# A decoder on one Trainium2 core: in the first attention, masks and sinks are copied into the score banks by ACT and VectorE

## The chip, the core and the metric

The kernel runs on one core of a Trainium2 chip, as one program. The metric is device time in microseconds of one execution; the median of several runs is compared. Engines are named as in the profile: PE is the matmul engine (PEld its weight loads), DVE is VectorE, ACT is ScalarE, POOL is GpSimd, SP issues DMAs.

## What is computed

Two decoder layers on x of shape (8, 112, 512), each with a self-attention, a cross-attention and a feed-forward part, all with a layer norm ahead and a residual. The change concerns the self-attention of the first layer only:

```python
H, KV, D = (32, 8, 64)
G = H // KV
WINDOW = 64
...
scale = D ** (-0.5)
scores = jnp.einsum('bhqd,bhkd->bhqk', q, k) * scale
i = jnp.arange(Tq)
mask = (i[None, :] > i[:, None]) | (i[:, None] - i[None, :] >= WINDOW)
scores = jnp.where(mask[None, None], -jnp.inf, scores)
sink_col = jnp.broadcast_to(sinks[None, :, None, None], (Bq, H, Tq, 1))
combined = jnp.concatenate([scores, sink_col], axis=-1)
probs = jax.nn.softmax(combined, axis=-1)[..., :-1]
out = jnp.einsum('bhqk,bhkd->bhqd', probs, v)
```

So a row of scores has 112 keys, of which some are masked, and one extra column, the head's sink.

## The kernel before, in words

The program is written engine by engine. Each engine runs its own list of stages in order (projections, first attention, its output projection, cross-attention and so on), and instructions wait on semaphores that count in the order of the engine that raises them. `done(...)` names a point that an instruction raises, `upon(...)` a point that is waited for. An engine has one counter for a stage, so `act_a0` counts all of ACT's points in the first attention.

**Tiling of the first attention.** There are U0 = 32 units of eight heads for one batch element, and W0 = 16 rounds w of two units, 2w and 2w+1 (a batch element takes two rounds). The score banks are PSUM banks 0 to 3: unit 2w uses banks 0 and 1, unit 2w+1 banks 2 and 3. Each bank holds four heads with 114 columns each, 112 scores and two columns for the sink (the softmax reads the first of them). Banks 4 and 5 take transposed probabilities, 6 and 7 the value products. So there is one set of score banks: round w+1 can touch them only after the exp of round w has read them.

**A round on PE** (`pe_att0`). `scores(w)` first writes the mask into each of the four banks (L532, an identity matmul with start=True, which overwrites), waiting for the exp of the unit that used the bank last (L531). Then come eight matmuls with one row each that put the sinks, split into a high and a low part, into the two last columns (L536), and 64 products of 32 rows, Q by K (L542), which add to the mask. After the scores PE transposes unit 2w-3 (`turn`, eight transposes, L260), makes the value products of unit 2w-4 (`values`, L566), subtracts the row maxima of unit 2w from its banks with two matmuls (`less`, L550), transposes unit 2w-2, subtracts those of unit 2w+1, and makes the value products of unit 2w-3. In rounds 0 and 1 some value projections (L255 to L257) stand between. The order of this list is fixed by hand.

**The other engines.** DVE takes the maxima of both units (`largest`, L650), then the sums of the exps (`sums`, L655, and a reciprocal, L657), for the even unit in its own round and for the odd one at the start of the next. ACT raises exp (`power`, L612) into SBUF tiles Sk, copies transposed probabilities to SBUF (`turned`, L604) and value products to QO (`out`, L618); in rounds 2 and 3 it also rounds a weight piece (L296) between the two exps. POOL multiplies Sk by the reciprocals (`share`, L677). Before the stage, `dve_proj0` scales the sinks by 8, copies a row of ones and splits the sinks into skh and skl; ACT copies the identity (`one`, L621) and the mask (`maskR`, L622) to fp32r tiles for PE. The value add of the projection stage is L398.

The last two rounds (w = 16, 17) make no scores; they finish the transposes and value products. Then the output projection (L255 to L257) follows on PE.

Of the kernel before, what the change touches and what calls it, by code (L numbers as in the profile page):

```python
# [8 lines left out]
F = mybir.dt.float32  # L9
# [66 lines left out]
def build(nc, g):  # L76
# [8 lines left out]
    with ExitStack() as ctx:  # L85
# [56 lines left out]
        ones = misc("ones", [128, S], R)  # L142
        skh = misc("skh", [S, 32], R)
        skl = misc("skl", [S, 32], R)
# [290 lines left out]
        def dve_proj0(e):  # L435
# [25 lines left out]
            e.tensor_scalar(M("sinks", S), M("sinks", S), 8.0, None, A.mult).then_inc(*done("dve_p0", "sinks8"))  # L461
            e.tensor_copy(ones[:, :], C("ones")[:, 0:S]).then_inc(*done("dve_p0", "ones"))
            e.wait_ge(*upon("dve_p0", "sinks8"))
            e.tensor_copy(skh[:, :], M("sinks", S)).then_inc(*done("dve_p0", "skh"))
            e.wait_ge(*upon("dve_p0", "skh"))
            e.tensor_tensor(skl[:, :], M("sinks", S), skh[:, :].bitcast(F), A.subtract).then_inc(*done("dve_p0", "sinks"))
# [42 lines left out]
        def sinks_of(part, w, i):  # L509
            row = part[32 * i:32 * i + 1, :].rearrange("p (s h i) -> p s i h", s=2, h=4)[:, w % 2, i, :]  # L510
            return row.unsqueeze(2).to_broadcast([1, 4, 2])
# [15 lines left out]
        def pe_att0(e):  # L527
            def scores(w):
                b, s = w // 2, w % 2
                for i in range(4):  # L530
                    e.wait_ge(*(upon("act_a0", "exp", 2 * w - 2 + i // 2) if w else upon("dve_p0", 16 + i // 2, i % 2)))  # L531
                    e.matmul(bank0(i)[:, :, 0:S], one[0:S, 0:S], maskR[:, :].unsqueeze(1).to_broadcast([S, 4, S]), start=True,  # L532
                             stop=True)
                for part in (skh, skl):
                    for i in range(4):
                        e.matmul(bank0(i)[:, :, S:S + 2], ones[32 * i:32 * i + 1, :], sinks_of(part, w, i), start=False, stop=True,  # L536
                                 skip_group_check=True)
                for h in range(4):
                    for ab in range(2):
                        for i in range(4):  # L540
                            p = slice(32 * i, 32 * i + 32)
                            last = e.matmul(bank0(i)[:, h, 0:S], QO[p, 1 + w, 2 * h + ab, :],  # L542
                                            Kt[p, 2 * s + ab, b * S:(b + 1) * S], start=False, stop=True, skip_group_check=True)
                            if h == 3 and ab == 1:
                                last.then_inc(*done("pe_a0", "sc", w, i))
# [25 lines left out]
            e.wait_ge(*upon("act_a0", "mask"))  # L571
            e.wait_ge(*upon("dve_p0", "sinks"))
# [26 lines left out]
        def act_att0(e):  # L599
# [20 lines left out]
            e.wait_ge(*upon("pe_ln", "x", NT - 1))  # L620
            e.activation(one[:, :], C("ident"), ACT.Copy)  # L621
            e.activation(maskR[:, :], C("mask0", S), ACT.Copy).then_inc(*done("act_a0", "mask"))  # L622
            for w in range(W0 + 2):
# [9 lines left out]
                if w < W0:  # L633
                    power(2 * w + 1)
                if 0 < w <= W0:
                    turned(2 * w - 2)
# [7 lines left out]
        def dve_att0(e):  # L644
# [6 lines left out]

            def sums(u):
# [5 lines left out]

            for w in range(W0 + 1):
                if w:  # L660
                    sums(2 * w - 1)
                if w < W0:
                    largest(2 * w)
                    largest(2 * w + 1)
                    if w < 2:
                        value0_out(e, 6 + w)
                    sums(2 * w)
# [1909 lines left out]
```

## Time and profile before

| | us |
|---|---|
| median of 3 runs | 1678.25 |
| lowest and highest | 1677.41 and 1680.61 |
| the profiled execution, its time | 1680.23 |
| its span, first to last instruction | 1678.4 |
| PE busy | 1602.4 |
| DVE busy | 991.4 |
| ACT busy | 730.2 |
| POOL busy | 508.6 |

The span is read from the profile, which is one execution; its busy times overlap, since the engines work side by side. The first attention runs from 138.2 us (its first mask matmul) to about 267 us, where the output projection's matmuls begin. A row of the timeline merges instructions of one kind that follow each other: its duration is that of the group, and its count stands behind the x.

### The profile page before, as it was taken

The numbers are of one execution on the slowest core, as the hardware profiler recorded it, in microseconds if no ns is written. First come the engines' busy times: TensorE is split into PE (matmuls) and PEld (weight loads), VectorE is DVE, ScalarE is ACT, GpSimd is POOL, SyncE is SP. The second block draws the span as 40 slices with busy tenths as digits, with TensorE's granted clock in tenths as the row PEclk, the third lists the DMA queues.
The fourth block names the chain that finished last, engine by engine and source line by source line (L and its number), as shares of the span: only waits on it lengthen the run. The fifth ranks groups of instructions, "written<-read, shape, count | busy, mean of one in ns | idle before, by whom it ended". The sixth has DMA issues, their size and how long they took to land.

```text
span 1678.4 us, 24116 instructions
## 1 busy us (share of the span) xinstructions
PE 1602.4 (95%) x9668; PEld 1329.3 (79%) x9668; DVE 991.4 (59%) x1658; ACT 730.2 (44%) x1221; POOL 508.6 (30%) x335
## 2 busy tenths in 40 slices
PE   7999999999899999989999989999889999999998
PEld 6897667778688888867889987787677888878887
DVE  5555663455676675487758748244757455554555
ACT  2113664223577765666611146422635334353442
POOL 3875542520100002331117734111611432212321
PEclk9999999999999999999999999999999999999999
DMA  4110003134312004410001110110001111111111
GB/s 164 53 61 28 2 2 130 39 99 130 106 53 64 13 1 161 156 38 1 1 1 63 50 39 1 44 43 32 21 14 44 51 53 55 51 45 51 51 57 44
DMA packets 28578, 88.49 MB, mean 53 GB/s; under 512 B 4154, under 2 KB 4282, under 8 KB 28215
## 3 DMA queue, kind: packets, MB, share of 16 engines
q1 hardware_dynamic: 28468, 86.96, 15.6%
q8 instruction: 77, 1.26, 0.3%
q14 instruction: 33, 0.27, 0.1%
HBM read 85.11 MB, written 1.84 MB: 52 GB/s over the span
## 4 chain that ended last, share of the span: by engine, by line
PE 85%; DVE 8%; ACT 4%; issue 1%; POOL 0%; DMA 0%; ACTq 0%; DVEq 0%
PE PS L255 18%; PE PS L257 17%; PE PS L256 17%; PE PS L260 6%; PE PS L1026 5%; PE PS L1044 4%; PE PS L1376 3%; PE PS L932 3%; PE PS L1391 2%; PE PS L542 2%; PE PS L566 1%; PE PS L1623 1%; PE PS L1611 1%; PE PS L532 1%; DVE sm L1645 1%
## 5 line engine op out<-in xcount | busy, mean ns | idle before, releaser
L301 POOL TENSOR_TENSOR HL<-stg,HL 128x1024 fp32r<-128x1024 f32 (+2 forms) x111 | 244.0, 2201 | 824.2 <-ACT HL L296 803.8
L255 PE MATMUL PS<-XT,HL 128*128 128x448 f32 x608 | 225.3, 371 | 7.5 <-DVE XT L336 5.3
L257 PE MATMUL PS<-XT,HL 128*128 128x448 f32 x608 | 223.5, 368 | 0.0
L256 PE MATMUL PS<-XT,HL 128*128 128x448 f32 x608 | 223.5, 368 | 0.0
L296 ACT ACTIVATE HL<-stg 128x1024 fp32r<-128x1024 f32 (+2 forms) x111 | 104.2, 943 | 217.8 <-PE PS L257 202.5
L255 PE MATMUL PS<-HL,XT 128*128 128x512 f32 (+1 forms) x380 | 138.6, 365 | 3.7 <-DVE rs L316 1.6
L257 PE MATMUL PS<-HL,XT 128*128 128x512 f32 (+1 forms) x380 | 135.4, 356 | 0.0
L256 PE MATMUL PS<-HL,XT 128*128 128x512 f32 (+1 forms) x380 | 135.3, 356 | 0.0
L255 PEld LDWEIGHTS PS<-XT,HL 128*128 128x128 f32 x608 | 115.0, 189 | 19.1 <-DVE XT L336 6.0
L256 PEld LDWEIGHTS PS<-XT,HL 128*128 128x128 f32 x608 | 115.0, 189 | 9.7
L257 PEld LDWEIGHTS PS<-XT,HL 128*128 128x128 f32 x608 | 114.9, 189 | 9.8
L2197 DVE SCALAR_TENSOR_TENSOR Hh<-PS,sml,Hh 128x448 fp32r<-128x448 f32 x64 | 43.8, 684 | 114.2 <-ACT Hh L2085 114.2
L1026 PE MATMUL PS<-kvT,QO 128*112 128x375 f32 x256 | 93.2, 487 | 6.4 <-DVE kvT L816 5.6
L255 PE MATMUL PS<-HL,Ph 128*128 128x512 f32 x224 | 90.4, 404 | 5.4 <-DVE x L2227 1.8
L706 DVE TENSOR_TENSOR XT<-QO,XT 128x896 fp32r<-128x896 f32 x32 | 36.8, 1159 | 98.3 <-ACT XT L700 98.3
L1090 DVE TENSOR_REDUCE nm<-PS 112x2 f32<-112x750 f32 x64 | 60.1, 939 | 52.4 <-PE PS L1026 52.4
L256 PE MATMUL PS<-HL,Ph 128*128 128x512 f32 x224 | 87.5, 391 | 0.0
L257 PE MATMUL PS<-HL,Ph 128*128 128x512 f32 x224 | 87.5, 391 | 0.0
L2085 ACT ACTIVATE Hh<-PS,sml 128x448 fp32r<-128x448 f32 x64 | 40.6, 634 | 105.7 <-PE PS L257 105.7
L1044 PE MATMUL PS<-PX,kvr 125*128 125x224 f32 x384 | 84.2, 355 | 0.0
L255 PEld LDWEIGHTS PS<-HL,XT 128*128 128x128 f32 (+1 forms) x380 | 70.9, 187 | 16.0 <-issue 3.5
L257 PEld LDWEIGHTS PS<-HL,XT 128*128 128x128 f32 (+1 forms) x380 | 70.7, 186 | 10.4
(283 smaller groups left out, 3603.2 us busy)
## 6 DMA issues: line engine op xcount, KB each, us to landing
stg<-in_wst SPq DMA_DIRECT2D x87, 512.0 KB, 3.5
stg<-in_wst SPq DMA_DIRECT2D x16, 352.0 KB, 3.1
stg<-in_wst SPq DMA_DIRECT2D x16, 320.0 KB, 3.8
wsum<-in_wfc SPq DMA_DIRECT2D x8, 512.0 KB, 4.1
wsum<-in_wpj SPq DMA_DIRECT2D x8, 512.0 KB, 3.6
raw<-in_wfc SPq DMA_DIRECT2D x8, 512.0 KB, 6.7
stg<-in_wst SPq DMA_DIRECT2D x16, 256.0 KB, 2.6
raw<-in_wpj SPq DMA_DIRECT2D x7, 512.0 KB, 7.0
```

The lines of the kernel that those rows point to most:

```text
L255: e.matmul(out, lh, rh, start=start, stop=False)
L256: e.matmul(out, lh, rl, start=False, stop=False)
L257: return e.matmul(out, ll, rh, start=False, stop=stop)
L260: return e.transpose(out, in_, C("ident", n)[:, 0:n])
L296: e.activation(slot(k)[:, 0, 0:n], stg[k % NSTG][:, 0:n], ACT.Copy).then_inc(*done("act_w", k))
L301: e.tensor_tensor(slot(k)[:, 1, 0:n], stg[k % NSTG][:, 0:n], slot(k)[:, 0, 0:n].bitcast(F), A.subtract).then_inc(*done("pool_w", k))
L932: last = e.matmul(out, Mhl[i][:, a, kc, :], XT[:, c, kc, hs], start=kc == 0 and j == 0, stop=kc == 3 and j == 2)
L1026: last = e.matmul(PS[0:S, bank + e_, 0:L], QO[:, 1 + st // 4, 2 * (st % 4) + e_, :], kvT[:, b, :], start=True, stop=True)
L1044: last = e.matmul(PS[:, 6 + u % 2, 0:2 * S], kvr[:, c, u // 4 % 8, :], PX[u % 2][:, :, c, :], start=c == 0, stop=c == 2)
L1090: e.tensor_reduce(nm[:, st % 4, :], PS[0:S, bank:bank + 2, 0:L], AX.X, A.max, negate=True).then_inc(*done("dve_x", "nm", st))
L1376: last = e.matmul(PS[:, 7, :], YT[c4][:, hl, kc, :], w_rows(ter, 1, c4 * 4 + kc), start=c4 == 0 and kc == 0 and hl == 0, stop=c4 == 3 and ...
L2197: e.scalar_tensor_tensor(out=half_of(Hh[:, 1, ch, :], h), in0=PS[:, 2 * h + ch, 0:HT], scalar=M("bup")[:, 2 * n + ch:2 * n + ch + 1], in1= ...
```

## The change

The mask and the sinks are no longer put into the score banks by PE. ACT and DVE copy them there, in fp32, from the constant table (mask0) and from the scaled sinks: DVE banks 0 and 1 for the even unit, ACT banks 2 and 3 for the odd unit. A fill is two instructions, one of 896 elements a partition (2 banks, 4 heads, 112 columns) and one of 16 (the sink columns). It waits for the exp that read the banks last. In ACT's list it stands right behind the exp of the odd unit, ahead of the copy of transposed probabilities; in DVE's list behind the maxima of its round, ahead of the sums of the even unit. The score products wait for both fills, and are to add to what they find in the banks. Only once, ahead of round 0, PE writes all 456 columns of each of the four banks with start=True (`clear`); the first fills wait for that. The matmuls for masks and sinks go, and with them the tiles ones, skh and skl, DVE's instructions that made them, and ACT's copy of the mask.

```diff
--- before.py
+++ after.py
@@ -139,9 +139,6 @@
         rsl = misc("rsl", [P, 2, 8])
         nmr = misc("nmr", [S, 4, 8], R)
         one = misc("one", [128, 128], R)
-        ones = misc("ones", [128, S], R)
-        skh = misc("skh", [S, 32], R)
-        skl = misc("skl", [S, 32], R)
         nm = misc("nm", [S, 4, 2])
         sx = misc("sx", [S, 4, 2])
         rx = misc("rx", [S, 4, 2])
@@ -458,12 +455,7 @@
                     ln_lo(e, "x", t, t)
             rope0(e, 2)
             rope0(e, 3)
-            e.tensor_scalar(M("sinks", S), M("sinks", S), 8.0, None, A.mult).then_inc(*done("dve_p0", "sinks8"))
-            e.tensor_copy(ones[:, :], C("ones")[:, 0:S]).then_inc(*done("dve_p0", "ones"))
-            e.wait_ge(*upon("dve_p0", "sinks8"))
-            e.tensor_copy(skh[:, :], M("sinks", S)).then_inc(*done("dve_p0", "skh"))
-            e.wait_ge(*upon("dve_p0", "skh"))
-            e.tensor_tensor(skl[:, :], M("sinks", S), skh[:, :].bitcast(F), A.subtract).then_inc(*done("dve_p0", "sinks"))
+            e.tensor_scalar(M("sinks", S), M("sinks", S), 8.0, None, A.mult).then_inc(*done("dve_p0", "sinks"))
             for u in range(4, 20):
                 rope0(e, u)
             value0_out(e, 4)
@@ -506,9 +498,17 @@
 
         U0, W0, U1 = 32, 16, 16
 
-        def sinks_of(part, w, i):
-            row = part[32 * i:32 * i + 1, :].rearrange("p (s h i) -> p s i h", s=2, h=4)[:, w % 2, i, :]
-            return row.unsqueeze(2).to_broadcast([1, 4, 2])
+        def sinks_of(u):
+            i = 2 * (u % 2)
+            sk = M("sinks", S).rearrange("p (s h i) -> p s i h", s=2, h=4)[:, u // 2 % 2, i:i + 2, :]
+            return sk.unsqueeze(3).to_broadcast([S, 2, 4, 2])
+
+        def mask_of():
+            return C("mask0", S).unsqueeze(1).unsqueeze(1).to_broadcast([S, 2, 4, S])
+
+        def whole0(u):
+            i = 2 * (u % 2)
+            return PS[0:S, i:i + 2, 0:4 * S + 8].rearrange("p i (h k) -> p i h k", h=4)
 
 
         def keys(ap, h=4):
@@ -527,14 +527,8 @@
         def pe_att0(e):
             def scores(w):
                 b, s = w // 2, w % 2
-                for i in range(4):
-                    e.wait_ge(*(upon("act_a0", "exp", 2 * w - 2 + i // 2) if w else upon("dve_p0", 16 + i // 2, i % 2)))
-                    e.matmul(bank0(i)[:, :, 0:S], one[0:S, 0:S], maskR[:, :].unsqueeze(1).to_broadcast([S, 4, S]), start=True,
-                             stop=True)
-                for part in (skh, skl):
-                    for i in range(4):
-                        e.matmul(bank0(i)[:, :, S:S + 2], ones[32 * i:32 * i + 1, :], sinks_of(part, w, i), start=False, stop=True,
-                                 skip_group_check=True)
+                e.wait_ge(*upon("dve_a0", "fill", 2 * w))
+                e.wait_ge(*upon("act_a0", "fill", 2 * w + 1))
                 for h in range(4):
                     for ab in range(2):
                         for i in range(4):
@@ -568,8 +562,11 @@
                 last.then_inc(*done("pe_a0", "pv", u))
 
             e.wait_ge(*upon("pool_p0", 19, 1))
-            e.wait_ge(*upon("act_a0", "mask"))
-            e.wait_ge(*upon("dve_p0", "sinks"))
+            e.wait_ge(*upon("act_a0", "one"))
+            for i in range(4):
+                e.wait_ge(*upon("dve_p0", 16 + i // 2, i % 2))
+                e.matmul(bank0(i), one[0:S, 0:S], one[0:S, 0:S + 2].unsqueeze(1).to_broadcast([S, 4, S + 2]), start=True,
+                         stop=True).then_inc(*done("pe_a0", "clear", i))
             for w in range(W0 + 2):
                 if w < W0:
                     scores(w)
@@ -617,9 +614,16 @@
                 g = 4 * (u % 2)
                 e.activation(QO[:, u // 2, g:g + 4, :], psv(6 + u % 2), ACT.Copy).then_inc(*done("act_a0", "o", u))
 
-            e.wait_ge(*upon("pe_ln", "x", NT - 1))
-            e.activation(one[:, :], C("ident"), ACT.Copy)
-            e.activation(maskR[:, :], C("mask0", S), ACT.Copy).then_inc(*done("act_a0", "mask"))
+            def fill(u):
+                if u > 1:
+                    e.wait_ge(*upon("act_a0", "exp", u - 2))
+                e.activation(whole0(u)[..., 0:S], mask_of(), ACT.Copy)
+                e.activation(whole0(u)[..., S:S + 2], sinks_of(u), ACT.Copy).then_inc(*done("act_a0", "fill", u))
+
+            e.activation(one[:, :], C("ident"), ACT.Copy).then_inc(*done("act_a0", "one"))
+            e.wait_ge(*upon("dve_p0", "sinks"))
+            e.wait_ge(*upon("pe_a0", "clear", 3))
+            fill(1)
             for w in range(W0 + 2):
                 if w > 1:
                     turned(2 * w - 3)
@@ -632,6 +636,8 @@
                     o_hi(e, "o0", 0)
                 if w < W0:
                     power(2 * w + 1)
+                if w < W0 - 1:
+                    fill(2 * w + 3)
                 if 0 < w <= W0:
                     turned(2 * w - 2)
                 if w >= W0:
@@ -649,6 +655,12 @@
                 e.wait_ge(*upon("pe_a0", "sc", u // 2, 2 * (u % 2) + 1))
                 e.tensor_reduce(nmr[:, k, :], unit0(u), AX.X, A.max, negate=True).then_inc(*done("dve_a0", "mx", u))
 
+            def fill(u):
+                if u:
+                    e.wait_ge(*upon("act_a0", "exp", u - 2))
+                e.tensor_copy(whole0(u)[..., 0:S], mask_of())
+                e.tensor_copy(whole0(u)[..., S:S + 2], sinks_of(u)).then_inc(*done("dve_a0", "fill", u))
+
             def sums(u):
                 k = u % 4
                 e.wait_ge(*upon("act_a0", "exp", u))
@@ -656,12 +668,16 @@
                 e.wait_ge(*upon("dve_a0", "sum", u))
                 e.reciprocal(rc[:, k, :], sm[:, k, :]).then_inc(*done("dve_a0", "rc", u))
 
+            e.wait_ge(*upon("pe_a0", "clear", 1))
+            fill(0)
             for w in range(W0 + 1):
                 if w:
                     sums(2 * w - 1)
                 if w < W0:
                     largest(2 * w)
                     largest(2 * w + 1)
+                    if w < W0 - 1:
+                        fill(2 * w + 2)
                     if w < 2:
                         value0_out(e, 6 + w)
                     sums(2 * w)
```

## Rows read from the trace of the kernel before

**Rows 1.** The page's first part: busy us of each engine.
```profile
PE 1602.4 (95%) x9668; PEld 1329.3 (79%) x9668; DVE 991.4 (59%) x1658; ACT 730.2 (44%) x1221; POOL 508.6 (30%) x335
```

**Rows 2.** Windows: stretch, length, busy us by engine (instructions), granted clock, DMA.
```profile
177.00:251.16 74.16, 74.16 (x1042) 49.73 (x1040) 45.91 (x61) 45.06 (x61) 33.25 (x20) 1.00 0.01 2
1210.00:1220.00 10.00, 8.14 (x131) 6.13 (x131) 7.21 (x12) 7.03 (x10) 4.03 (x3) 1.00 0.01 2
1220.00:1230.00 10.00, 5.51 (x88) 4.32 (x88) 2.31 (x4) 4.40 (x6) 3.32 (x2) 0.83 0.01 2
```

**Rows 3.** Timeline of one steady round: start us, duration, engine, line, operation, idle before.
```profile
208.01 1.81 PE L542 MATMUL PS<-Kt,QO 32*112 32x112 f32 x64
...
209.97 2.11 DVE L650 TENSOR_REDUCE nmr<-PS 112x8 fp32r<-112x904 f32 x2 [1.57 <-PE PS L542]
...
212.04 0.93 PE L260 MATMUL PS<-cst,Sk 112*112 112x112 f32 x8
212.30 0.92 ACT L612 ACTIVATE Sk<-PS 112x904 f32<-112x904 f32 x1
...
212.74 0.62 PE L550 MATMUL PS<-nmr,one 112*112 112x456 f32 x2
213.26 1.09 DVE L655 TENSOR_REDUCE sm<-Sk 112x8 f32<-112x904 f32 x1 [1.19 <-ACT Sk L612]
...
213.46 0.92 ACT L612 ACTIVATE Sk<-PS 112x904 f32<-112x904 f32 x1 [0.23 <-PE PS L550]
...
214.19 1.07 PE L532 MATMUL PS<-maskR,one 112*112 112x448 f32 x4
214.28 0.91 ACT L604 ACTIVATE PT<-PS 112x896 f32<-112x896 f32 x1
214.39 0.20 DVE L657 RECIPROCAL rc<-sm 112x8 f32<-112x8 f32 x1
214.51 1.04 DVE L655 TENSOR_REDUCE sm<-Sk 112x8 f32<-112x904 f32 x1
214.67 3.32 POOL L677 TENSOR_TENSOR Sk<-Sk,rc 112x896 f32<-112x896 f32 x2 [4.06 <-DVE rc L657]
...
215.41 1.81 PE L542 MATMUL PS<-Kt,QO 32*112 32x112 f32 x64
215.58 0.21 DVE L657 RECIPROCAL rc<-sm 112x8 f32<-112x8 f32 x1
```

**Rows 4.** Groups by form: copies on ACT and DVE; busy us, mean ns, idle before.
```profile
L700 ACT ACTIVATE XT<-QO 128x896 fp32r<-128x896 f32 x32 | 30.2, 950 | 74.5 <-PE PS L257 74.4
...
L621 ACT ACTIVATE one<-cst 128x128 fp32r<-128x128 f32 x1 | 0.3, 292 | 0.0
...
L1105 DVE COPY QO<-PS 128x224 f32<-128x224 f32 x64 | 25.1, 392 | 5.3 <-PE PS L1044 4.6
...
L1000 DVE COPY QO<-PS 128x448 f32<-128x448 f32 x16 | 9.3, 615 | 0.4 <-PE PS L954 0.4
L1461 DVE TENSOR_SCALAR Gb<-Gb,rs 128x2048 f32<-128x2048 f32 x7 | 9.0, 1286 | 0.2
```

**Rows 5.** Timeline of the start, round 0 and the end of round 2.
```profile
138.19 0.97 PE L532 MATMUL PS<-maskR,one 112*112 112x448 f32 x4
138.38 0.69 DVE L398 TENSOR_TENSOR V<-PS,bv 112x512 f32<-112x512 f32 x1 [2.14 <-PE PS L257]
...
139.31 1.81 PE L542 MATMUL PS<-Kt,QO 32*112 32x112 f32 x64
...
144.56 1.74 ACT L612 ACTIVATE Sk<-PS 112x904 f32<-112x904 f32 x2 [9.03 <-PE PS L550]
...
147.16 1.81 PE L542 MATMUL PS<-Kt,QO 32*112 32x112 f32 x64
...
161.44 0.92 ACT L612 ACTIVATE Sk<-PS 112x904 f32<-112x904 f32 x1
...
163.21 1.81 PE L542 MATMUL PS<-Kt,QO 32*112 32x112 f32 x64
```

## Prediction

> **What bounds the kernel now.** I read the page's head first: PE is busy 1602.4 of 1678.4 us and nothing else comes near it [rows 1]. That says only that PE matters on average, so I went to the stage that the change edits, the first attention. The windows view of its steady stretch, 177.00 to 251.16 us, shows PE busy all 74.16 us, at granted clock 1.00, while DVE is busy 45.9 and ACT 45.1 [rows 2]. So in these rounds PE never rests, and work taken off it is worth something, until another thing ends the round.
>
> What that other thing is has to be read from one round, in the timeline [rows 3]. A round w starts with its score products (208.01) and the next round's start at 215.41: 7.40 us. Count from 208.01 as zero. PE issues the 64 score products, eight transposes, four value products, the two matmuls that take off unit 2w's maxima, eight more transposes (212.04), and then, at 4.73, the two for unit 2w+1 (212.74 in the row). They last 0.62. ACT then makes exp(2w+1) from 5.45 to 6.37 (213.46, 0.92 long). PE in the meantime does value products, and at 214.19, 6.18 on this scale, begins the four mask matmuls of the next round, then the sinks' eight, then the scores. The masks of the banks that exp(2w+1) read can be written just after that exp ended at 214.38, so the exp-to-scores link is 215.41 - 214.38 = 1.03 us. The mask and sink matmuls fill this link almost completely. The round has two limits that lie close together: PE's list, 7.40 long, and the loop scores, maxima, subtraction, exp, bank ready, scores, which is just as long because the bank is made ready inside it.
>
> **The change part by part.**
>
> Removed from PE: 12 matmuls in each of 16 rounds, 215.41 - 214.19 = 1.22 us a round, 19.5 us in all. PE's own list falls to about 6.2 us. If PE alone set the pace, this would be the gain.
>
> Added to the loop: the fill. The bank pair of unit 2w+1 may be written only after exp(2w+1) has read it, and the scores of round w+1 wait for the copy. Before, the same bank pair was made ready by PE after the same exp; now it is made ready by ACT after it. The wait that vanishes (PE on its own list) is replaced by PE waiting for two ACT copies.
>
> Price of ACT's two copies. No row before shows ACT writing a score bank. The nearest rows are ACT copies of the same size from SBUF to SBUF, 896 elements in 950 ns, and one of 128 in 292 ns [rows 4]: 0.857 ns an element, so 16 elements take 292 - 112 x 0.857 = 196 ns. Two ACT instructions without a wait between them overlap: exp starts at 213.46, the next at 214.28, 0.82 later, though it lasts 0.92 [rows 3]. So the pair takes 0.95 - 0.10 + 0.20 = 1.05 us. An engine sees another's or its own end 0.04 later (exp(2w) ends 213.22, DVE starts 213.26; a sum ends 214.35, its reciprocal starts 214.39 [rows 3]). The new link is 0.04 + 1.05 + 0.05 = 1.14 us against 1.03. I take SBUF-to-SBUF as the price because the source is SBUF. Low bound: the big copy like the 0.82 that a PSUM read of that size occupies, the small one at half its estimate, 0.10: link 1.01. High bound: no overlap and a small copy as dear as the 128-element one: 0.95 + 0.29 + 0.09 = 1.33.
>
> [...]
>
> Added to DVE: a copy pair a round for unit 2w+2. The nearest rows are copies of 448 elements in 615 ns and 224 in 392 [rows 4], 0.996 ns an element: 896 take 1.06 us and 16 take 0.18, 1.25 together. The low bound is the paired pace of the 2048-element row, 1286 ns or at most 0.63 ns an element, some 0.75 for both. It starts after exp(2w), at 5.25, and is done at 6.5, a full microsecond before ACT's. Queued behind it on DVE are the sums of unit 2w, their reciprocals and the sums of 2w+1, which took 213.26 to 215.78 (two reduces, 1.13 and 1.07 with their gaps, and a reciprocal each); now they end at 6.5 + 2.5 = 9.0, that is 1.5 into the next round, and the first maxima reduce is wanted at 1.96 (209.97) [rows 3]. Slack 0.46. POOL's shares (3.32 for two) start at 7.8 in place of 6.66 (214.67) and end 11.1; PE transposes the first of them in the next round at 7.5 + 4.0 = 11.5 (212.04 is that place in the row). So DVE's fill costs nothing; it would need to last 1.7 us before it did.
>
> Queued behind ACT's fill are the copy of transposed unit 2w-2 (214.28 in the row) and an output copy: they move 1.1 later, to end about 1.3 into the next round. The first of them is wanted by PE at 1.8, when its scores are out. Nothing.
>
> Steady rounds: the 11 from 4 to 14 grow by 1.14 - 1.03 = 0.11, together 1.2 us.
>
> The four transitions before these lose more, since there the link was shorter: in round 0 both exps end at 144.56 + 1.74 = 146.30 and the scores start at 147.16, 0.86; in round 2 a weight copy on ACT pushes exp to 161.44, it ends 162.36, scores start 163.21, 0.85 [rows 5]. I take 0.86 for all four: 4 x (1.14 - 0.86) = 1.1 us.
>
> The start. Four new matmuls of 456 columns replace the first four of the masks, 138.19 to 139.16 [rows 5]: no change. But now the fills stand between them and the first scores, which before started at 139.31. ACT can start at 139.2, and is done at 140.3; DVE first finishes the value add (138.38 + 0.69) and is done at about 140.35. Scores start at 140.4: 1.1 us later, once. ACT's table load for Exp moves behind the first fill and ends long before the first exp at 144.56, so it is hidden. The three small DVE instructions that go (two copies and a subtract) lie in the projection under PE's work: nothing.
>
> The last round has no fill behind it, so the tail is as before. Sum: 1.2 + 1.1 + 1.1 = +3.4 us. The profiled execution has a span of 1678.4 and took 1680.23, so it would become 1681.8 and 1683.6; the median of the runs, 1678.25, lies 2.0 below that execution, and becomes 1681.7. All of the 19.5 us turns into PE waiting.
>
> **The rivals.**
>
> B, the short link: ACT's writes cost their low bound, 1.01. Then 11 x -0.02 + 4 x 0.15 + 0.9 = 1.3 us, 1679.6, not slower. It decides on where the pair takes under 0.95. For it: ACT reads PSUM faster than SBUF. Against: the source stays SBUF. Chance 0.17. [...]
>
> C, the clock: PE now rests 1.2 us in every 7.5, 83% busy. Where PE was 81% busy the clock still stood at 1.00, where it was 55% busy it was 0.83 [rows 2]. Should it be 0.83 here, PE's 5.4 us inside the loop stretch by 1.1, times 15 is 16 us on top of the 3.4: 1698. Chance 0.06.
>
> D, the removed PE time comes back at least in part: some step of the loop shortens when PE is less loaded, say by 0.5 us a round: 15 x 0.5 less the 3.4 is 4.1, so 1674. Nothing in the rows speaks for it: the subtraction of unit 2w+1 is placed by PE's order after the scores, which is unchanged, and even an ACT copy at the 0.63 ns of DVE's paired pace would leave the link at about 0.9 and the time at 1678. But a loop read from one engine's starts can be misread. Chance 0.10.
>
> That the copies don't survive (products overwrite them instead of adding) would not move the time.
>
> **How the numbers follow.** The forecast has 0.67: 1681.7, itself from 1680.5 to 1685. High bound of the link: 11 x 0.30 + 4 x 0.47 + 1.4 = 6.6, so 1684.9. The range goes from 1676, into D, past B, to 1687, the high bound and the 2 us by which runs of this kernel spread; C and D are out. A measurement can tell about 0.2%, 3.4 us, from no change; the forecast sits on that bound, so I split it 0.39 slower and 0.28 the same. With B the same has 0.45, with C slower has 0.45, D is faster 0.10.
>
> **What would show it.** Right: the period of the scores at 7.5, PE idle about 1.2 us before each, released by ACT; ACT's big copy near 0.95, the small one 0.2; first scores at about 140.4; DVE's maxima still starting 1.96 after the scores. Wrong: a period under 7.3, or scores released by DVE, or a clock under 1.00 in the stage.

## The result, and the profile after

| | before | after |
|---|---|---|
| median of the runs, us | 1679.43 (4 runs, 1677.41 to 1682.8) | 1691.46 (4 runs, 1690.99 to 1692.44) |
| profiled execution, its time | 1680.23 | 1691.88 |
| its span | 1678.4 | 1690.1 |
| first bank matmul to first output-projection matmul | 138.19 to 266.99, 128.80 | 136.58 to 276.16, 139.58 |
| PE busy | 1602.4 | 1590.0 |

The changed kernel is slower: the ratio of the times is 1.0071, with a 95% interval of 1.0058 to 1.0083. The forecast was 1681.7 with a range of 1676 to 1687, so the time lies 4.5 us above the range. Nearly all of it lies in the stage that the change edits: it is 10.78 us longer in the profiled execution, and the whole execution 11.65.

The first part of the profile's page (busy us of each engine) answers to [rows 1]:

```profile
PE 1590.0 (94%) x9480; PEld 1323.8 (78%) x9480; DVE 1006.1 (60%) x1687; ACT 746.9 (44%) x1252; POOL 508.7 (30%) x335
```

PE has 12.4 us less work, not the 19.5 that were taken out. About 1.0 is the new clearing of the banks. The rest, some 6 us, is work that was always there and now takes longer, all of it within the stage: outside it PE is busy 1477.1 us before and 1476.7 after.

The windows view (stretch, length, busy us by engine, granted clock, DMA) shows where. The first four windows lie around the starts of rounds 1 to 4, each with some idle time ahead of the scores, the last in the steady rounds, to be held against [rows 2]:

```profile
145.00:150.00 5.00, 3.02 (x64) 3.02 (x64) 4.12 (x7) 1.80 (x3) 1.93 (x2) 0.66 0.00 0
155.00:160.00 5.00, 3.11 (x64) 3.10 (x64) 3.70 (x7) 2.55 (x4) 2.35 (x2) 0.67 0.02 3
165.00:170.00 5.00, 3.42 (x66) 3.26 (x67) 2.42 (x5) 2.67 (x5) 3.87 (x2) 0.69 0.01 3
175.00:180.00 5.00, 3.64 (x70) 3.48 (x71) 2.83 (x5) 2.45 (x5) 4.09 (x3) 0.71 0.01 3
190.00:252.00 62.00, 51.45 (x746) 34.33 (x746) 45.48 (x65) 45.27 (x66) 26.60 (x16) 1.00 0.01 2
```

In the kernel before, the same four windows have a granted clock of 1.00. Here it averages 0.66 to 0.71, between levels of 0.50 (as from 146.43 to 149.80 us) and 1.00, and returns to 1.00 for the steady rounds, though PE is busy only 83% of them (51.45 of 62).

The timeline of PE's score products, one row a round from round 0 to 5 (start, duration, engine, line, operation, count, idle time before it and what ended that):

```profile
138.86 1.84 PE L536 MATMUL PS<-Kt,QO 32*112 32x112 f32 x64 [1.27 <-ACT PS L621]
...
146.98 3.17 PE L536 MATMUL PS<-Kt,QO 32*112 32x112 f32 x64 [2.59 <-ACT PS L621]
...
156.89 3.33 PE L536 MATMUL PS<-Kt,QO 32*112 32x112 f32 x64 [2.16 <-ACT PS L621]
...
166.57 3.10 PE L536 MATMUL PS<-Kt,QO 32*112 32x112 f32 x64 [1.92 <-ACT PS L621]
...
176.36 2.69 PE L536 MATMUL PS<-Kt,QO 32*112 32x112 f32 x64 [1.93 <-ACT PS L621]
...
185.55 1.84 PE L536 MATMUL PS<-Kt,QO 32*112 32x112 f32 x64 [1.32 <-ACT PS L621]
```

The same 64 products take 1.84 us after an idle time of 1.3 us, and 2.7 to 3.3 after one of 1.9 to 2.6. All idle times end by ACT's small copy, L621, as the change makes them. The profiled execution isn't alone in this: the mean granted clock of a whole execution is 0.986 or 0.987 in all four runs of the changed kernel, and 0.988 to 0.993 in the 57 runs of the kernel before that stood beside the experiments. So three things are to be told apart: the link itself, the longer idle times of rounds 0 to 3, and the clock behind them.

One link of the steady rounds, to be held against [rows 3]:

```profile
213.62 1.09 DVE L661 COPY PS<-cst 112x896 f32<-112x896 f32 x1 [1.23 <-ACT Sk L609]
...
213.81 0.92 ACT L609 ACTIVATE Sk<-PS 112x904 f32<-112x904 f32 x1 [0.23 <-PE PS L544]
214.62 0.17 DVE L662 COPY PS<-sml 112x16 f32<-112x16 f32 x1
...
214.77 0.92 ACT L620 ACTIVATE PS<-cst 112x896 f32<-112x896 f32 x1
215.62 0.17 ACT L621 ACTIVATE PS<-sml 112x16 f32<-112x16 f32 x1
...
215.94 1.84 PE L536 MATMUL PS<-Kt,QO 32*112 32x112 f32 x64 [1.32 <-ACT PS L621]
...
217.88 2.10 DVE L656 TENSOR_REDUCE nmr<-PS 112x8 fp32r<-112x904 f32 x2 [0.67 <-PE PS L536]
```

The exp ends at 213.81 + 0.92 = 214.73. ACT's copies run from 214.77 to 215.79, and the scores start at 215.94: a link of 1.21 us, of which 0.15 lies between the last copy's end and the scores. The round lasts 7.60 us (208.34 to 215.94).

The groups of instructions by form (busy us, mean ns of one, idle before them) give the prices of the new copies:

```profile
L661 DVE COPY PS<-cst 112x896 f32<-112x896 f32 x16 | 17.5, 1095 | 21.4 <-ACT Sk L609 21.4
L620 ACT ACTIVATE PS<-cst 112x896 f32<-112x896 f32 x16 | 14.7, 921 | 5.6 <-PE PS L568 5.2
L621 ACT ACTIVATE PS<-sml 112x16 f32<-112x16 f32 x16 | 2.7, 169 | 0.0
L662 DVE COPY PS<-sml 112x16 f32<-112x16 f32 x16 | 2.7, 168 | 0.0
```

### The profile page after: what moved, and what is told of

Read it like the earlier page. It is cut to its first block, busy times and chain, and to the rows that moved or that the text cites. A ratio compares the mean times of both kernels' runs of the same rounds, so it can differ in the third digit from the quotient of the medians.

```text
span 1690.1 us, 23816 instructions
## 1 busy us (share of the span) xinstructions
PE 1590.0 (94%) x9480; PEld 1323.8 (78%) x9480; DVE 1006.1 (60%) x1687; ACT 746.9 (44%) x1252; POOL 508.7 (30%) x335
## 3 DMA queue, kind: packets, MB, share of 16 engines
q8 instruction: 76, 1.25, 0.3%
HBM read 85.11 MB, written 1.84 MB: 51 GB/s over the span
## 4 chain that ended last, share of the span: by engine, by line
PE 83%; DVE 8%; ACT 5%; issue 2%; DMA 0%; POOL 0%; SPq 0%; ACTq 0%; DVEq 0%
PE PS L252 17%; PE PS L254 17%; PE PS L253 17%; PE PS L257 6%; PE PS L1042 5%; PE PS L1060 4%; PE PS L1392 3%; PE PS L948 3%; PE PS L1407 2%; PE PS L536 2%; PE PS L1639 1%; PE PS L1627 1%; ACT Sk L609 1%; DVE sm L1661 1%; PE PS L544 1%
```

## The experiments

Two theories stood at first. **Theory G**: the link costs what it costs, and beyond it the long idle times of rounds 0 to 3 let PE's clock fall. **The rival**: the products themselves are slow for another reason, such as products that add to copied contents, or engines that write banks beside PE. A fall, below, is a drop of the granted clock to 0.50. The lengths given below are those of the stage, from the first matmul into a score bank to the first of the output projection (128.80 before, 139.58 after), and the period is the distance between the scores of steady rounds (7.39 before over 11 of them, 7.60 after). Diffs are against the changed kernel, those of gap, before_early and mixed2_early against the kernel before. The number of runs stands behind each time; each kernel has one profiled execution, and f0, gap and one_wait have no other.

**Idle times filled (f03).** PE gets matmuls into a bank that nobody reads then, at the end of rounds 0 to 3, behind a wait for that bank to be free. Nothing else differs from the changed kernel.

```diff
+        FILL = {0: 11, 1: 9, 2: 8, 3: 8}
...
+            def filler(w, n):
...
+                for _ in range(n):
+                    e.matmul(PS[0:S, 6 if w else 4, 0:4 * S], one[0:S, 0:S],
+                             one[0:S, 0:S].unsqueeze(1).to_broadcast([S, 4, S]), start=True, stop=True)
...
                 if w > 1:
                     values(2 * w - 3)
+                if w in FILL:
+                    filler(w, FILL[w])
```

> The changed kernel with filler matmuls (448 columns, into a bank nobody uses at that moment) in PE's waiting time after rounds 0 to 3: 11, 9, 8, 8 of them. Theory (the idle gap of 1.9 to 2.6 us ahead of the scores takes PE's clock to its lower level): scores of rounds 1 to 4 back from 3.1-3.3 to 1.84 us, granted clock 1.00 through the stage, 6 us less than the changed kernel, about 1685.5. Rival (the scores of these rounds are slow because ACT or DVE write or read banks beside them, or because products add to data that another engine wrote): they stay at 3.1-3.3 and the time stays at 1691 or rises.

Measured: 1685.2 us (6 runs), ratio to before 1.0038 [1.0022, 1.0055]. The stage is 133.63. Windows around the starts of rounds 1 and 2, and the scores of round 1:

```profile
145.00:150.00 5.00, 4.65 (x83) 4.03 (x82) 4.93 (x9) 1.65 (x3) 2.08 (x2) 1.00 0.00 0
155.00:160.00 5.00, 4.67 (x85) 3.56 (x85) 4.34 (x6) 2.83 (x6) 3.33 (x2) 1.00 0.00 0
```

```profile
146.82 1.84 PE L548 MATMUL PS<-Kt,QO 32*112 32x112 f32 x64 [0.35 <-ACT PS L635]
```

The scores of rounds 1 to 4 all take 1.84 us, at clock 1.00, though they add to the same copied contents beside the same engines. PE has 36 matmuls more and the kernel is 6.3 us faster. That decides for the clock: with work whose results nobody uses it is granted at 1.00 through the whole stage, and the stage is 5.95 us shorter (133.63 against 139.58).

**Only the first idle time filled (f0).** The diff is that of f03 with `FILL = {0: 11}`.

> The same with the filler after round 0 alone. Theory (each gap lowers the clock by itself): round 1's scores 1.84 us, rounds 2, 3 and 4 still slow, 1.5 us less than the changed kernel, 1690. Rival (the fall after round 0 starts a chain that keeps the next rounds slow): with the first gap filled all four are quick, 1685.5.

Measured: 1684.06 us in one run, stage 135.26. Its score rows of rounds 2, 3 and 4:

```profile
155.94 1.84 PE L548 MATMUL PS<-Kt,QO 32*112 32x112 f32 x64 [2.16 <-ACT PS L635]
...
164.14 2.17 PE L548 MATMUL PS<-Kt,QO 32*112 32x112 f32 x64 [1.92 <-ACT PS L635]
...
173.90 1.84 PE L548 MATMUL PS<-Kt,QO 32*112 32x112 f32 x64 [1.92 <-ACT PS L635]
```

Neither case that I had written came out. Round 2 ran its scores in 1.84 us behind an idle time of 2.16, round 4 behind 1.92, and round 3 slowed behind 1.92. That one fall made the round 9.77 us long against 8.20 in f03. So idle times that went with a fall in the changed kernel sometimes pass without one, and round 3 fell though round 2 had not.

**An idle time in the kernel before (gap).** ACT makes copies that nobody uses ahead of the exps, two in round 0 and four in round 8. PE fills the banks itself, as before.

```diff
+                if w in (0, 8):
+                    e.wait_ge(*upon("pe_a0", "sub", 2 * w))
+                    for j in range(2 if w == 0 else 4):
...
+                        e.activation(to, C("mask0", S).unsqueeze(1).to_broadcast([S, 8, S]), ACT.Copy).then_inc(*done("act_a0", "pad", w, j))
                 if w < W0:
                     power(2 * w)
```

> The kernel before, masks and sinks by PE as ever, with idle copies on ACT ahead of the exps of round 0 (two, 1.7 us) and of round 8 (four, 3.3 us), so that PE waits about 2.3 us ahead of the next masks; nothing is filled by ACT or DVE. Theory (a gap on PE lowers its clock, whatever else runs): the scores of round 1, round 9 or both take 3.1 us in place of 1.81, granted clock 0.7 to 0.8 over these 5 us. Rival (the slow scores belong to banks that ACT and DVE fill): both stay at 1.81 us.

Measured: 1690.25 us in one run. The first masks after each of the two idle times, and the scores behind them:

```profile
147.42 0.67 PE L532 MATMUL PS<-maskR,one 112*112 112x448 f32 x2 [3.87 <-ACT Sk L612]
...
149.63 3.31 PE L542 MATMUL PS<-Kt,QO 32*112 32x112 f32 x64
...
214.12 0.66 PE L532 MATMUL PS<-maskR,one 112*112 112x448 f32 x2 [2.31 <-ACT Sk L612]
...
215.74 1.81 PE L542 MATMUL PS<-Kt,QO 32*112 32x112 f32 x64
```

The first idle time became 3.87 us, longer than meant, because a table load of 1.28 us came between the copies and the exps. Behind it the scores took 3.31 us and the clock stood at 0.50 from 148.3 to 155. Behind 2.31 us in round 8 they took 1.81, at clock 1.00. So an idle PE alone, with no fill by ACT or DVE anywhere, can halve the clock; the rival is out. But 2.31 us behind long dense work didn't do it, in this one run.

**ACT's fill alone (act_odd), and DVE's alone (dve_even).** PE makes masks and sinks for the even unit's banks in the first kernel and for the odd unit's in the second; the other pair is filled as in the changed kernel. The first one's scores:

```diff
             def scores(w):
                 b, s = w // 2, w % 2
-                e.wait_ge(*upon("dve_a0", "fill", 2 * w))
+                for i in (0, 1):
+                    if w:
+                        e.wait_ge(*upon("act_a0", "exp", 2 * w - 2 + i // 2))
+                    e.matmul(bank0(i)[:, :, 0:S], one[0:S, 0:S], maskR[:, :].unsqueeze(1).to_broadcast([S, 4, S]), start=True,
+                             stop=True)
...
                 e.wait_ge(*upon("act_a0", "fill", 2 * w + 1))
```

> Half of the change: ACT fills the odd unit's banks, PE writes masks and sinks of the even unit's banks as before, DVE fills nothing. Theory: the loop still runs through ACT's fill, so the steady period is 7.6 us as in the changed kernel; PE's gap is cut in two pieces (the even banks' matmuls, 0.6 us, stand in it), so the clock stays up in most or all of rounds 1 to 4: 1685 to 1687. Rival (DVE's fill is what costs): period 7.4, time at the kernel before's 1679.

> The other half: DVE fills the even unit's banks, PE writes masks and sinks of the odd unit's after exp. Theory: ACT's fill leaves the loop, the link from exp to scores falls from 1.21 to about 0.6 us, the steady period is 7.0 us, no gap over 1 us, clock at 1.00: 15 x 0.4 less 1.1 at the start, 1674. Rival (DVE's fill is the bound, through the sums behind it): period 7.4 or more, 1680 or slower.

Measured: act_odd 1683.47 us (9 runs), ratio 1.0032 [1.0016, 1.0048], stage 132.45, period 7.50. dve_even 1681.48 (10 runs), ratio 1.0006 [0.9992, 1.0021], stage 129.39, period 7.22.

With ACT's fill alone PE's idle time is cut in pieces by its own masks (what is left ahead of the scores is 0.92 to 1.27 us in rounds 1 to 4 and 0.36 in the steady ones), the clock stays at 1.00 throughout the stage, and the time is below what I expected. The period is 7.50 rather than 7.60: PE waits for one engine ahead of its scores and not for two.

With DVE's fill alone I had expected 1674 and a period near 7.0. The link of dve_even, in the timeline:

```profile
206.46 0.92 ACT L630 ACTIVATE Sk<-PS 112x904 f32<-112x904 f32 x1 [0.23 <-PE PS L564]
...
207.43 0.67 PE L545 MATMUL PS<-maskR,one 112*112 112x448 f32 x2 [0.17 <-ACT Sk L630]
208.03 0.26 PE L549 MATMUL PS<-skh,ones 1*112 1x8 f32 x2
...
208.23 1.82 PE L556 MATMUL PS<-Kt,QO 32*112 32x112 f32 x62
```

The exp ends at 207.38 and the scores, but for two of the 64, run from 208.23: 0.85 us, with two masks where four stood. I had halved the link. Two things keep it longer. The matmuls from the first mask to the scores take 0.80 us where twice as many took 1.22, and in the kernel before the first masks, those of the even banks, began 0.19 ahead of the exp's end (214.19 against 214.38 in [rows 3]), while here they begin 0.05 behind it. Besides, the clock fell in round 1 there too: its masks begin after 1.44 us of idle time, its scores take 3.28, and it lasts 9.79, where I had expected a clock of 1.00. What remains is a kernel that can't be told from the one before.

**The order on PE (before_early, after_early).** If PE waits in a loop, the second subtraction could be issued earlier. Both kernels take `less(2 * w + 1)` ahead of the transposes of unit 2w-2; the first is otherwise the kernel before, the second the changed one.

```diff
                 if w < W0:
                     less(2 * w)
+                    less(2 * w + 1)
                 if 0 < w <= W0:
                     turn(2 * w - 2)
-                if w < W0:
-                    less(2 * w + 1)
```

> The kernel before with one reordering on PE: the subtraction of unit 2w+1 ahead of the transposes of unit 2w-2. It shortens the loop through exp by about 0.5 us and leaves PE's list as long. Theory (PE's list of 7.4 us is what bounds the rounds of the kernel before): period 7.4 to 7.5, time 1679 within 2. Rival (the loop bounds it too): period about 6.9, 1672.

> The changed kernel with the same reordering. Theory (the loop through exp and ACT's fill bounds it, PE's list of 6.2 us does not): period 7.6 falls by 0.5 to about 7.1, 10 x 0.5 and some of the first rounds' gaps: 1682 to 1686. Rival (another thing, DVE or the copies themselves, holds the period): 7.6 stays and so does 1691.

Measured: before_early 1682.33 us (10 runs), ratio 1.0021 [1.0011, 1.0031], stage 129.98, period 7.56. after_early 1688.83 (4 runs), ratio 1.0055 [1.0040, 1.0069], stage 135.24, period 7.26. So the reorder alone makes the old stage 1.2 us longer and not shorter: PE's list is its bound, and now it waits for the second maxima on top (this row is PE's weight load for that subtraction):

```profile
211.56 0.27 PEld L550 LDWEIGHTS PS<-nmr,one 112*112 112x112 f32 x2 [0.29 <-DVE nmr L649]
```

Neither theory gave this: the period is above 7.4 to 7.5, let alone 6.9, and the time above 1679 within 2. The stage accounts for 1.2 of the 4 us between the medians; on the rest see the open points below.

In the changed kernel the same reorder takes 0.34 us off each steady round, because there the loop is the bound. It missed the expected time, since the steady rounds gave 0.34 and not 0.5 and three of the first rounds still fell: scores of 3.34, 2.85 and 2.45 us behind 2.59, 1.64 and 1.93 us of idle time. The first of these falls held through the whole of round 1, which lasted 11.03. One idle time of 1.82 in it passed without a fall.

**The fills from round 4 on (late).** PE makes masks and sinks for rounds 0 to 3, ACT and DVE from then on, and the clearing goes.

```diff
             def scores(w):
                 b, s = w // 2, w % 2
+                if w < 4:
...
+                else:
+                    e.wait_ge(*upon("dve_a0", "fill", 2 * w))
+                    e.wait_ge(*upon("act_a0", "fill", 2 * w + 1))
...
-                if w < W0 - 1:
+                if 3 <= w < W0 - 1:
                     fill(2 * w + 3)
```

> The change from round 4 on: in rounds 0 to 3 PE writes masks and sinks of all banks as in the kernel before, from round 4 on ACT and DVE fill them. No clearing matmuls, no fill ahead of the first scores. Theory (the start costs 1.1 us, the gaps of rounds 0 to 3 cost 6 us by the clock and 1.1 us by the longer link, the later rounds 0.2 us each): rounds 0 to 3 as before, 7.60 from round 4 on, clock at 1.00, 11 or 12 x 0.2 = 2.3 us slower than the kernel before, 1681. Rival (fills lower the clock wherever they begin): a fall in rounds 4 to 7, 1686.

Measured: 1684.65 us (10 runs), ratio 1.0028 [1.0017, 1.0038], stage 133.00. Scores of rounds 4 and 5, and the window on the first:

```profile
169.20 2.63 PE L558 MATMUL PS<-Kt,QO 32*112 32x112 f32 x64 [1.93 <-ACT PS L640]
...
178.35 1.84 PE L558 MATMUL PS<-Kt,QO 32*112 32x112 f32 x64 [1.32 <-ACT PS L640]
```

```profile
170.00:175.00 5.00, 5.00 (x60) 3.73 (x53) 2.10 (x2) 1.72 (x3) 4.38 (x3) 0.66 0.01 5
```

Rounds 0 to 3 begin where the kernel before has them (7.85, 8.22 and 7.83 apart), so their loss in the changed kernel comes from the fills. The one idle time of 1.93 us left, where ACT has both a weight piece and a fill ahead of PE's scores, costs a fall, and round 4 lasts 9.15; those of 1.32 behind it don't. Neither case as written came out: not a clock of 1.00 throughout, and not falls in rounds 4 to 7, but one in round 4.

**One wait on PE in place of two (one_wait).** Where do the 0.15 us ahead of the scores come from? PE's wait for DVE's fill moves to ACT, between its two copies; DVE is long done by then.

```diff
             def scores(w):
                 b, s = w // 2, w % 2
-                e.wait_ge(*upon("dve_a0", "fill", 2 * w))
                 e.wait_ge(*upon("act_a0", "fill", 2 * w + 1))
...
                 e.activation(whole0(u)[..., 0:S], mask_of(), ACT.Copy)
+                e.wait_ge(*upon("dve_a0", "fill", u - 1))
                 e.activation(whole0(u)[..., S:S + 2], sinks_of(u), ACT.Copy).then_inc(*done("act_a0", "fill", u))
```

> The changed kernel, but PE waits for ACT's fill alone ahead of its scores; ACT waits for DVE's fill, long done, between its two copies. The same copies and order otherwise. Theory (PE starts 0.14 us after the last copy rather than 0.05 because it has two waits there): period 7.60 falls to 7.51. Rival (that lateness belongs to a copy into PSUM or to an engine that stood idle): 7.60 stays.

Measured: 1694.45 us in one run, stage 138.35, period 7.50. The end of ACT's small copy to the scores:

```profile
210.14 0.17 ACT L621 ACTIVATE PS<-sml 112x16 f32<-112x16 f32 x1
...
210.37 1.84 PE L535 MATMUL PS<-Kt,QO 32*112 32x112 f32 x64 [1.23 <-ACT PS L621]
```

The distance is 0.06 instead of 0.15, and the round 0.10 shorter. So a second wait on PE, satisfied long before, costs about 0.10 us when it stands with the one that ends last; act_odd, which has one wait there too, has the same period. The time of this single run is not lower for it: the stage is 1.2 shorter, and the rest of the execution longer (its stage starts at 139.19, that of after at 136.58). The falls in rounds 1 to 4 are as in the changed kernel.

**What follows for a better kernel (mixed2_early, mixed2).** The pieces say: a fill is worth something if it takes PE's list below 7.40 while PE still has the matmuls that bridge the link, and only with the second subtraction issued early. So DVE fills the even banks from round 2 on, PE makes the odd ones (and all in rounds 0 and 1), ACT fills none, the clearing goes, and the reorder above is in. mixed2 is the same without the reorder.

```diff
             def scores(w):
                 b, s = w // 2, w % 2
+                banks = (2, 3) if w > 1 else (0, 1, 2, 3)
...
+                if w > 1:
+                    e.wait_ge(*upon("dve_a0", "fill", 2 * w))
...
+                    if 0 < w < W0 - 1:
+                        fill(2 * w + 2)
```

> DVE fills the even unit's banks from round 2 on, PE writes masks and sinks of the odd unit's banks (and of all banks in rounds 0 and 1, so no clearing and no fill ahead of the first scores), and the same reordering. Theory: link from exp to scores 0.85 us, loop 4.3 + 0.6 + 0.1 + 0.9 + 0.85, about 6.8; PE's list 7.4 less 0.5, 6.9; period 6.9 to 7.0, no gap over 1 us, clock at 1.00: 14 x 0.45 less than the kernel before, 1673. Rival (DVE's longer list, 5.9 us plus waits, takes over): period 7.2 or more, 1677.

> DVE fills the even unit's banks from round 2 on, PE makes the rest, order of PE as in the kernel before. Theory (a link of 0.85 us from exp to scores, set by the odd banks' masks and sinks): period 7.22 from round 4 on, 11 or 12 x 0.17 = 2 us faster than before, 1677, between no change and 0.2%. Rival (PE's shorter list counts in full): period 6.9, 1674.

> The combination of the earlier run once more, beside the version without the reordering on the same chip: period 7.00, 1673 to 1674, 0.3 to 0.4% faster than the kernel before; the reordering alone had given none of it (1682).

Measured: mixed2_early 1673.73 us (5 runs), ratio 0.9963 [0.9948, 0.9977], and in a second comparison 1673.75 (6 runs), 0.9957 [0.9944, 0.9971]. mixed2 1680.37 (12 runs), 1.0001 [0.9990, 1.0012]. Steady rounds of mixed2_early, and the work around its exps:

```profile
177.00:246.00 69.00, 69.00 (x976) 45.98 (x972) 54.87 (x79) 42.80 (x60) 33.24 (x20) 1.00 0.01 2
```

```profile
202.20 1.74 ACT L626 ACTIVATE Sk<-PS 112x904 f32<-112x904 f32 x2
...
204.11 0.66 PE L545 MATMUL PS<-maskR,one 112*112 112x448 f32 x2
...
204.89 1.82 PE L557 MATMUL PS<-Kt,QO 32*112 32x112 f32 x62
```

PE is busy all the time again, the clock is 1.00 in the whole stage, and the period is 6.99 against 7.40; the stage takes 123.74 against 128.80. The exps end at 203.94, 0.95 before the scores, and PE has value products until its masks begin. mixed2's stage is 1.94 shorter than that of the kernel before (126.86, period 7.22), yet its median doesn't show it; its runs spread from 1674.15 to 1682.59. Its granted clock over the whole execution was 0.990 or less in 9 of the 12 runs, against 9 of 22 for the kernel before beside it. Among the runs at 0.991 or more the medians are 1677.59 (3 runs) against 1678.16, among the others 1680.97 against 1682.39. So at like clock there is a gain, from too few runs to size it. That of mixed2_early holds in the same way: among the runs at 0.991 or more its medians are 1671.54 (3 runs) against 1678.36, and in the second comparison 1673.56 (5 runs) against 1678.16.

## Why the prediction was wrong

The prediction had the direction right and the size wrong: +3.4 us forecast, 12.0 measured between the medians. The step that failed is the clock, a term put at nothing in the sum because PE's rest was taken as 1.2 us in every round. The 10.78 us of the stage come apart as follows; f03 gives the same rounds at full clock.

| part | predicted | measured | from |
|---|---|---|---|
| start of the stage | 1.1 | 1.16 | first bank matmul to first scores, 2.28 against 1.12 |
| first four transitions, at full clock | 1.1 | 1.40 | f03: 8.12, 8.61, 8.21, 8.20 against 7.85, 8.22, 7.83, 7.84 |
| 11 steady rounds | 1.2 | 2.3 | 7.60 against 7.39, each 0.21 |
| clock in rounds 1 to 4 | 0 | 5.95 | 9.91, 9.68, 9.79, 9.19 against f03's 8.61, 8.21, 8.20, 7.60 |

**The bound and the loop: right.** The score period was set by the link once PE's masks were gone. 19.5 us of PE work went and none of it shortened a steady round; PE idles before each and is released by ACT. That DVE's fill costs nothing held as well: it lasted 1.17 us of start-to-end in place of 1.25, the maxima start 1.94 after the scores (1.96 in [rows 3]), and DVE idles 0.67 ahead of them. ACT's later copies cost nothing either: over the stage PE waits 1.7 us for them ahead of its transposes, before as after.

**The link: right in kind, too short by one term.** ACT's pair was put at 1.05 and took 1.02 (214.77 to 215.79). The passage from the last copy to the scores was put at 0.05, from rows where an engine waits for one semaphore; with two it took 0.15, which one_wait shows. That makes the link 1.21 for 1.14. The steady rounds cost 2.3 us for 1.2, 1.1 of it by the second wait (11 x 0.10), while the cheaper copies and small shifts in the scores even out; the first four transitions cost 1.4 for 1.1, as 4 x (1.21 - 0.86) gives. On the price of the copy: ACT took 0.92 us for 896 elements into PSUM against 0.95 for SBUF to SBUF [rows 4], 0.03 less, though these two rows also differ in partitions (112 and 128) and output type. Rival B had for it that ACT reads PSUM faster, 0.91 us against 0.95 for 896 elements [rows 3, 4], two rows that differ in the same way; it needed a pair under 0.95 and didn't get it. The 1680.5 at which the forecast's own span begins lies 1.2 us below it, about what 0.04 us off each of ACT's 32 copies gives, the difference between those two reads. No row had ACT write a score bank, so that was an estimate; in the changed kernel the copies took 0.92 and 0.17 us in place of 0.95 and 0.20, 0.03 less each.

**The clock: the step that failed.** I priced rival C by PE's mean busy share, 83% in the steady rounds, held against two windows in [rows 2], and gave it 0.06. The sum had no term for it. For the steady rounds that reading was right: at 83% the clock stayed at 1.00. But the prediction says "PE now rests 1.2 us in every 7.5", and that holds only from round 4 on. In round 0 the two exps run as a pair, and PE has no transposes or value products to do meanwhile. The timeline of PE in the kernel before gave this, in two rows that I had not used (start, duration, count, idle time before it):

```profile
143.98 0.93 PE L550 MATMUL PS<-nmr,one 112*112 112x456 f32 x4
145.54 1.48 PE L532 MATMUL PS<-maskR,one 112*112 112x448 f32 x4 [0.63 <-ACT Sk L612]
```

The subtractions end at 144.91, the exps at 144.56 + 1.74 = 146.30 [rows 5], and a link of 1.14 puts the scores at 147.4, with 2.5 us in which PE has nothing. 2.59 was measured. The kernel before had the same hole, but its masks of the even banks began in it, after 0.63 us. Rounds 1 to 3 came out at 2.16, 1.92 and 1.93, where I had spread the same 1.2. So the removed masks were PE's first work in these idle stretches (in rounds 1 to 3 they began after 0.49, 0.19 and 0.18 us), and I priced what they take, not what they cover. The mechanism was on the list, but as a loss in all 15 rounds (16 us) and not in the four with long idle times (6 us).

The second window of [rows 2] was misread as well. Its 0.83 is no level of the clock but a mean: the clock was 1.00 up to 1226.6 and 0.50 from 1226.7 on. What PE did around that moment, with the window behind it:

```profile
1225.07 0.95 PE L260 MATMUL PS<-cst,Sb 112*112 112x112 f32 x8 [1.16 <-ACT PT L1856]
1227.09 1.72 PE L1820 MATMUL PS<-PT,V 112*32 112x112 f32 x32 [1.07 <-ACT PT L1856]
```

```profile
1226.70:1230.00 3.30, 1.72 (x32) 1.32 (x32) 0.55 (x1) 1.44 (x3) 0.00 (x0) 0.50 0.02 5
```

Idle times of 1.20, 1.07 and 1.16 us, with 1 to 2 us of matmuls between them, came ahead of the fall, and it began in the fourth, of 1.07. PE did less there than in a steady round, but the kernel before thus showed the clock falling around idle times no longer than the 1.2 us forecast for every round, and the mean over ten microseconds hid both the idle times and the level.

**What was missed in size** is then 5.95 us of clock, 1.1 in the second wait and 0.3 in the four transitions, of 7.4 in the stage; outside the stage the profiled executions differ by 0.9 (1549.6 and 1550.5), which is less than they vary from kernel to kernel (1545.5 to 1554.3).

**Open.** Which idle times lower the clock isn't settled. In the steady rounds of this stage 1.32 or less never did, but in the later stage above four of about 1.1 close together did. Among the early rounds falls went with idle times of 1.44, 1.64, 1.83, 1.92, 1.93, 2.07, 2.16, 2.50, 2.59 and 3.87, while others of 1.82, 1.92 and 2.16 passed, as did 2.31 in round 8 of a dense stage. The length alone doesn't decide it. Nor does the fall begin at a fixed distance from the idle time. Windows ahead of and behind the falls around the scores of rounds 1 and 4 in the changed kernel:

```profile
144.39:146.40 2.01, 0.00 (x0) 0.00 (x0) 1.40 (x3) 1.98 (x3) 0.00 (x0) 1.00 0.00 0
146.43:149.80 3.37, 2.82 (x60) 2.85 (x64) 2.69 (x5) 0.41 (x2) 1.73 (x2) 0.50 0.00 0
170.33:177.10 6.77, 4.84 (x54) 2.87 (x56) 5.06 (x8) 5.99 (x9) 2.62 (x2) 1.00 0.00 1
177.16:180.50 3.34, 3.34 (x52) 3.00 (x44) 1.37 (x2) 0.32 (x1) 3.34 (x3) 0.50 0.02 5
```

In round 1 the clock fell 0.6 us before the scores began (146.98), in round 4 0.8 us after (176.36), with PE busy again; hence the 3.17 and 2.69 us of the same products. What sets the moment no run here separates.

What moves the rest of the program by some us from one kernel to the next is in part the same thing. Outside the stage the clock fell several times in every kernel, and the profiled execution's length there goes with it: 1545.5 us in mixed2, where it stood at 0.50 for 24 us in all, 1549.6 in the kernel before with 31, 1554.3 in one_wait with 41. The kernel before, run 57 times beside the experiments, has a median of 1678.0 us in the 37 runs with a granted clock of 0.991 or more, and of 1682.5 in the other 20. This is also where before_early's median comes from: 9 of its 10 runs are at 0.990 or less, with a median of 1682.45. So a few us between two medians can come from the rest of the program, and the stage lengths are the better witness here. Why the rest falls more often in one kernel than in another stays open; outside the stage mixed2 differs from the kernel before in one wait of ACT alone, ahead of its copy of the identity.

## What to carry to other kernels

Before moving work off a busy engine, ask what that work covers. Here PE's matmuls filled the wait between the exp and the scores, and the copies that replaced them on another engine stand in the same wait, after the same event, so PE gained only idle time, 1.32 us in a steady round. Work out each idle time by itself, the first rounds of a pipeline above all, where little else is in flight; a mean busy share hides the few long ones (four here, of 1.92 to 2.59 us) behind which PE's clock stood at 0.50. A share of the work can be worth moving where all of it is not: here half the fills, to the engine with slack, plus the order that lets PE use the time, made the kernel 0.4% faster.

## What was not expected of the hardware

- Two waits on PE ahead of one matmul cost about 0.10 us more than one, although DVE's had been satisfied 1.0 us before ACT's (0.15 against 0.06 from the last copy's end to the scores).
- PE's clock fell from 1.00 to 0.50 around idle times between 1.44 and 3.87 us in rounds 1 to 4, and the scores of 1.84 us then took up to 3.3; idle times of 1.32 us, once in each of 11 rounds in a row, left it at 1.00, while four of 1.07 to 1.20 us within 8.3 us, in a later stage of the kernel before, went with a fall.
- The fall can begin within the idle time (0.6 us before PE's next matmul, round 1 of the changed kernel) or after PE is busy again (0.8 us in round 4).
- The same kernel before ran in 1678.0 or 1682.5 us (medians of 37 and 20 runs), by whether its mean granted clock was at least 0.991 or not.
- 36 matmuls without use made the kernel 6.3 us faster (1685.2 against 1691.46) and its stage 5.95.
- DVE copied 896 fp32 elements from SBUF into PSUM in 1095 ns and 16 in 168, 1.05 ns an element, with no sign of the 0.63 that [rows 4] show for 2048 elements within SBUF.
